# Splitting Wq and normalising the first rows in the context stage, and placing the first unit's maxima among the query projections

## The reference

```python
x = x + attn(layernorm(x), k, v, ...)                  # one head, 2048 keys
x = x + xattn(layernorm(x), ctx, ctx, Wq, bq, Wk, bk, Wv, bv, Wo, bo, mask)
x = x + ffn(layernorm(x), ...)                         # shared expert and top 2 of 8

# xattn: 16 heads of 32; ctx has 4 x 1601 rows
q, k, v = heads(Q @ Wq.T + bq), heads(K @ Wk.T + bk), heads(V @ Wv.T + bv)
scores = where(mask == 0, -1e9, q @ k.T / sqrt(32))
out = (softmax(scores) @ v) @ Wo.T + bo
```

## Time and profile before

| what | us |
|---|---|
| median of 3 runs | 4144.37 |
| lowest, highest | 4143.46, 4153.04 |
| the profiled execution | 4149.81 |
| its span in the trace | 4148.0 |
| TensorE busy | 3834.7 (92%) |
| VectorE busy | 2428.6 (59%) |
| ScalarE busy | 1427.9 (34%) |
| GpSimd busy | 1473.0 (36%) |

### The profile page before, as it was taken

One profiled execution on the slowest core, in us unless ns is written; L12 is line 12 of the kernel. 1 busy time (PEld: TensorE's weight loads), 2 busy tenths in 40 slices (PEclk: granted clock), 3 DMA queues, 4 the chain that ended last, 5 costly groups with the idle time before them and its releaser, 6 DMA issues. The chain is left out here.

```text
span 4148.0 us, 64160 instructions
## 1 busy us (share of the span) xinstructions
PE 3834.7 (92%) x19160; PEld 2567.8 (62%) x19161; DVE 2428.6 (59%) x6243; ACT 1427.9 (34%) x1752; POOL 1473.0 (36%) x806
## 2 busy tenths in 40 slices
PE   4999999979968699999999999999996799997997
PEld 3888888868856344444444444444442677785875
DVE  5444444434437488888878888878883533434235
ACT  2212211222222055455545554545554221212332
POOL 1000000000000177766666666777664212310033
PEclk7999999989988699999999999999998899998999
DMA  3010010045544412222222222222201433228478
GB/s 132 30 38 30 30 38 30 28 136 187 184 146 142 119 37 53 54 53 54 53 54 53 54 53 54 51 53 54 53 6 47 162 102 122 102 71 282 166 278 288
DMA packets 223679, 381.48 MB, mean 92 GB/s; under 512 B 16936, under 2 KB 101448, under 8 KB 223436
## 3 DMA queue, kind: packets, MB, share of 16 engines
q1 hardware_dynamic: 196204, 309.73, 25.6%
q0 software_dynamic: 13120, 43.00, 2.8%
q10 hardware_dynamic: 14112, 25.70, 1.6%
HBM read 229.71 MB, written 148.66 MB: 91 GB/s over the span
## 5 line engine op out<-in xcount | busy, mean ns | idle before, releaser
L1389 DVE CUSTOM_DVE_ANT_0 xa_unread<-xa_mx_ps,mask_q 128x402 bf16<-128x402 f32 x2048 | 1065.7, 573 | 330.2 <-PE xa_mx_ps L1249 192.8
L1356 ACT ACTIVATE xa_prob<-xa_scores 128x1024 f32<-128x1024 f32 (+1 forms) x832 | 834.2, 1023 | 821.6 <-PE xa_scores L1270 808.9
L1229 POOL TENSOR_TENSOR xa_sums<-xa_sums,xa_prob 128x1024 f32<-128x1024 f32 x448 | 1056.8, 2378 | 38.1 <-POOL xa_sums L1229 29.1
L1249 PE MATMUL xa_mx_ps<-xa_kp,xa_qp 96*128 96x402 f32 x2048 | 742.1, 428 | 34.9 <-DMA xa_vg<-values 34.8
L1249 PEld LDWEIGHTS xa_mx_ps<-xa_kp,xa_qp 96*128 96x128 f32 x2048 | 371.2, 192 | 382.7 <-DVE xa_maxima L1389 227.0
L1264 PE MATMUL xa_scores<-xa_qp,xa_kp 97*128 97x512 f32 (+1 forms) x1664 | 568.2, 423 | 14.5 <-issue 6.9
L1270 PE MATMUL xa_scores<-mask_t,ident_b 128*128 128x512 bf16 (+1 forms) x1664 | 549.8, 388 | 0.0
L1278 PE MATMUL xa_o_ps<-xa_prob,xa_vg 128*32 128x512 f32 (+1 forms) x3328 | 449.1, 606 | 3.7 <-issue 3.7
L1264 PEld LDWEIGHTS xa_scores<-xa_qp,xa_kp 97*128 97x128 f32 (+1 forms) x1664 | 296.5, 187 | 156.7 <-ACT xa_prob L1356 90.1
L1229 POOL TENSOR_TENSOR xa_sums<-xa_prob 128x1024 f32<-128x1024 f32 x64 | 151.1, 2380 | 532.3 <-ACT xa_prob L1356 532.3
L1270 PEld LDWEIGHTS xa_scores<-mask_t,ident_b 128*128 128x128 bf16 (+1 forms) x1664 | 122.9, 100 | 242.1 <-issue 207.9
(11 more groups left out here) (276 smaller groups left out, 6105.6 us busy)
## 6 DMA issues: line engine op xcount, KB each, us to landing
xa_kp<-kT_high SPq DMA_DIRECT2D x32, 800.5 KB
ex_src<-sorted_in SPq DMA_DIRECT2D x78, 256.0 KB
sorted_out<-ex_made ACTq DMA_DIRECT2D x78, 256.0 KB
xa_qp<-qT_high SPq DMA_DIRECT2D x32, 512.0 KB
xa_kp<-kT_low SPq DMA_DIRECT2D x16, 800.5 KB
cxl_rows<-in_ctx SPq DMA_DIRECT2D x16, 768.0 KB, 5.2
values<-cxl_v SPq DMA_DIRECT2D x48, 256.0 KB
xa_vg<-values SPq DMA_DIRECT2D x16, 768.0 KB
```

The source lines that it names most:

```text
L1229: pool.tensor_tensor(sums[pr][:, :, :], left[pr][:, :, :], right[pr][:, :, :], ALU.add).then_inc(pool_added, 1)
L1249: pe.matmul(mx_ps[slot % 3][:, 0:MKEYS], qp[par][0:MAXROW, j, first:first + P], kp[par][0:MAXROW, j, MFIRST[kb]:MFIRST[kb] + MKEYS], start ...
L1356: act.activation(prob[ring][pr][0:keys, :, :], scores[pr][0:keys, :, :], ACT.Exp, scale=SCALE).then_inc(exped, 1)
L1389: dve.tensor_tensor_reduce(out=unread[slot % 2][:, :], in0=mx_ps[slot % 3][:, 0:MKEYS], in1=mask_q[:, half * QB + qt, MFIRST[kb]:MFIRST[kb ...
```

## The change

Four things move. Wq is split in the context stage, in the same call as Wk and Wv; that function now waits for each weight by itself and goes around 8 banks. The first two steps' rows of x1 are loaded, and their statistics and normalisation done, in the last batch of the context stage. The query loop is written out instead of looped: it normalises in place in two row buffers, has two PSUM banks for turns instead of four, and gives the low parts of the queries to GpSimd. And the first unit of the cross attention is prepared there: keys and values are loaded at the start, its queries when they are stored, the 64 slots stand three to a chunk from step 2 on, with the reads on VectorE, two banks for them, and the peaks and the row behind. The cross attention then begins with its first score. Memory for the second unit's queries holds the parts of Wq, and two of the four sets of probabilities hold the rows.

```diff
 def split_weights(nc, ident, tag, weights, outs):
+        BANKS = min(len(weights) * DC, 8)
-                pe.wait_ge(loaded, 16 * len(weights))
                 for n, (w, r) in enumerate(cases):
+                    if r == 0:
+                        pe.wait_ge(loaded[w], 16)
+                    if n >= BANKS:
+                        pe.wait_ge(low_done, n - BANKS + 1)
...
 def context_keys_values(...)
-        split_weights(nc, ident, "cxw", [Wk, Wv], [wk, wv])
+        split_weights(nc, ident, "cxw", [Wk, Wv, Wq], [wk, wv, wq])
...
                     load(0, 0)
                     load(0, 1)
+                    for s in range(2):
+                        sp.dma_start(q_rows[s][:, :, :], x_rows[s]).then_inc(q_rows_in[s], 16)
...
                     def body(b, q, following):
                         low_k(b, q, following(1))
                         finish_v(b, q)
                         if q % 2 == 0:
                             preparation.vector(dve, 2 * b + q // 2)
+                        if isinstance(b, int) and q in (1, 2):
+                            normalize_queries(q - 1)
+                        if isinstance(b, int) and q in (0, 1):
+                            query_statistics(q)
```

In `cross_attention` the first loads, the first 64 slots and reads, `peak(0)`, `turn_peaks(0)`, `keep_row(0)` and `set_row(0, 0, 0)` are gone, the semaphores start from the values that they would have left, and GpSimd sets ones in one key buffer there, not two:

```diff
-                load(0, 0)
-                set_row(0, 0, 0)
                 later_loops(sp, unit)
...
-                pe.wait_ge(const, 3)
-                pe.wait_ge(loaded, 16 * LOADS)
-                for slot in range(SLOTS):
-                    mx(0, 0, 0, slot)
-                turn_peaks(0)
...
-                for slot in range(SLOTS):
-                    read(0, 0, slot)
-                peak(0)
```

More of the change, by code:

```diff
@@ L569, in split_weights @@
         rows = sb("rows", [P, len(weights), DC, D])
-        banks = ps("banks", [P, len(weights) * DC, DC, P])
-        loaded, turned, high_done, low_done = sem("loaded"), sem("turned"), sem("high"), sem("low")
+        BANKS = min(len(weights) * DC, 8)
+        banks = ps("banks", [P, BANKS, DC, P])
+        loaded = [sem(f"loaded{w}") for w in range(len(weights))]
+        turned, high_done, low_done = sem("turned"), sem("high"), sem("low")
         cases = [(w, r) for w in range(len(weights)) for r in range(DC)]
@@ L631, in context_keys_values @@
             preparation = MaskPreparation(sb, ps, sem, ident_b, mask, *masks)
+            norm = LayerNorm(sb, sem, BANK // P)
+            q_rows_in, normed = [sem(f"q_rows_in{i}") for i in range(2)], sem("normed")
+            x_rows = x1.rearrange("(s r p) n -> s p r n", p=P, r=BANK // P)
             def even(q):
@@ L720, in _ @@
                         pool.wait_ge(padded, n + 1)
+                    norm.pool_setup(pool)
+                    for s in range(2):
+                        norm.pool_step(pool, s)
                 @block.tensor
@@ L840, in _, with normalize_queries, query_statistics @@
                         low_c(0, 0, r)
+                    def normalize_queries(s):
+                        norm.normalize(dve, q_rows[s], q_rows[s], s).then_inc(normed, 1)
+                    def query_statistics(s):
+                        dve.wait_ge(q_rows_in[s], 16)
+                        norm.statistics(dve, q_rows[s], s)
                     def body(b, q, following):
@@ L1069, with load_keys @@
 PAIRS = GH // 2
-def cross_attention(nc, ident, ident_b, kT, qT, v, mask_q, mask_t, row, oT):
+QB = BANK // P
+MB, MKEYS = 4, 402
+MFIRST = [0, 400, 800, S2 - MKEYS]
+SLOTS = GH * QB * MB
+RING = 4
+MAXROW = 3 * DK
+ROWS97 = MAXROW + 1
+def load_keys(sp, kT, v, i, kp, vg, loaded):
+    for high_or_low, first in ((0, 0), (0, DK), (1, 2 * DK)):
+        sp.dma_start(words(kp[first:first + DK, :, :]),
+                     one(kT[high_or_low], i).rearrange("(j p) n -> p j n", p=DK)).then_inc(loaded, 16)
+    whole = (KT - 1) * P
+    sp.dma_start(vg[:, 0:KT - 1, :], one(v, i)[0:whole, :].rearrange("(t p) n -> p t n", p=P)).then_inc(loaded, 16)
+    sp.dma_start(vg[0:LAST, KT - 1, :], one(v, i)[whole:S2, :]).then_inc(loaded, 16)
@@ new lines, in load_queries, with put_row @@
+def load_queries(sp, qT, i, qp, queries, loaded):
+    for high_or_low, first in ((0, 0), (1, DK), (0, 2 * DK)):
+        sp.dma_start(words(qp[first:first + DK, :, queries]),
+                     one(qT[high_or_low], i).rearrange("(j p) n -> p j n", p=DK)[:, :, queries]).then_inc(loaded, 16)
+def put_row(sp, row, qp, half, row_in):
+    sp.dma_start(words(qp[MAXROW:ROWS97, :, half * BANK:(half + 1) * BANK]),
+                 row.rearrange("(o j t) n -> o j (t n)", o=1, j=GH)).then_inc(row_in, 16)
@@ new lines, in scores_of_slot, with maximum_of_slot @@
+def scores_of_slot(pe, out, qp, kp, half, slot):
+    j, qt, kb = slot // (QB * MB), slot // MB % QB, slot % MB
+    first = half * BANK + qt * P
+    return pe.matmul(out[:, 0:MKEYS], qp[0:MAXROW, j, first:first + P],
+                     kp[0:MAXROW, j, MFIRST[kb]:MFIRST[kb] + MKEYS], start=True, stop=True)
+def maximum_of_slot(dve, scores, mask_q, half, slot, unread, maxima):
+    j_qt, kb, qt = slot // MB, slot % MB, slot // MB % QB
+    return dve.tensor_tensor_reduce(
+        out=unread[slot % 2][:, :], in0=scores[:, 0:MKEYS],
+        in1=mask_q[:, half * QB + qt, MFIRST[kb]:MFIRST[kb] + MKEYS], scale=1.0, scalar=LOWEST,
+        op0=ALU.add, op1=ALU.max, accum_out=maxima[:, j_qt, kb:kb + 1])
@@ L1192, in set_row @@
                     sp.wait_ge(row_out, 16 * (u + 3))
[L1193 to L1194 removed]
+                    put_row(sp, row, qp[par], half, row_in)
                 def store(u, half):
@@ L1221, in _ @@
                 pool.memset(ones[:, :], 1.0).then_inc(const, 1)
-                for i in range(2):
-                    pool.wait_ge(const, i + 1)
-                    pool.memset(words(kp[i][MAXROW:ROWS97, :, :]), 1.0).then_inc(const, 1)
+                pool.wait_ge(const, 1)
+                pool.memset(words(kp[1][MAXROW:ROWS97, :, :]), 1.0).then_inc(const, 1)
+                pool.wait_ge(const, 2)
                 def add(u, kt, left, right):
@@ L1244, in mx @@
                 def mx(u, par, half, slot):
-                    j, qt, kb = slot // (QB * MB), slot // MB % QB, slot % MB
                     m = SLOTS * u + slot
                     pe.wait_ge(mx_read, m + 2)
-                    first = half * BANK + qt * P
-                    pe.matmul(mx_ps[slot % 3][:, 0:MKEYS], qp[par][0:MAXROW, j, first:first + P],
-                              kp[par][0:MAXROW, j, MFIRST[kb]:MFIRST[kb] + MKEYS], start=True, stop=True).then_inc(mx_made, 1)
+                    scores_of_slot(pe, mx_ps[slot % 3], qp[par], kp[par], half, slot).then_inc(mx_made, 1)
                 def turn_peaks(u):
@@ L1388, in read @@
                     dve.sem_inc(carried, 1)
-                    dve.tensor_tensor_reduce(
-           out=unread[slot % 2][:, :], in0=mx_ps[slot % 3][:, 0:MKEYS],
-           in1=mask_q[:, half * QB + qt, MFIRST[kb]:MFIRST[kb] + MKEYS], scale=1.0, scalar=LOWEST,
-           op0=ALU.add, op1=ALU.max, accum_out=maxima[:, j_qt, kb:kb + 1]).then_inc(mx_read, 1)
+                    maximum_of_slot(dve, mx_ps[slot % 3], mask_q, half, slot, unread, maxima).then_inc(mx_read, 1)
                 def peak(u):
```

400 lines of the change are left out of this document (201 added, 199 removed).

## The result

| what | before | changed |
|---|---|---|
| median of the runs | 4144.86 (4) | 4080.7 (4) |
| lowest, highest | 4143.46, 4153.04 | 4075.18, 4084.68 |
| profiled execution, its span | 4149.81, 4148.0 | 4079.72, 4077.9 |
| first score matmul in the trace | 1446.67 | 1383.11 |

The ratio is 0.984, 95% interval 0.9823 to 0.9858: 64.2 us less, against 66 forecast. The first score comes 63.6 us earlier, so the medians leave next to nothing to explain behind it. From the first score to the first hidden-layer product (L44 of `hdl_proj_ps`, at 3216.37 before and 3149.29 after) it is 1769.7 and 1766.2 us, and in two later runs 1768.7 and 1764.9: that much is the difference between executions. The two profiled spans are 70.1 us apart, and 6.5 of that lies behind the first score.

What follows compares the result with a forecast made beforehand. The kernel was taken as a chain of TensorE stages, with idle time from 1203.6 to 1446.67 to gain. Terms put the first score at 1380.1 instead of 1446.7, 66.6 us less: 4078 us, range 4061 to 4095.

Steps and rivals of the forecast that it cites:

- T0 moves: Start of the projection's block comes 6.9 us later, from Wq's split and LayerNorm work in the context stage; bounds 0.4 and 12.
- filling: Start of the projection's block: four turns with their high and low parts before the first products, 6.1 us.
- steps 0 and 1: First two projection steps: 14.4 us with a cold start, then 19.9 with a stall for late rows.
- wait for the queries: TensorE at slot 0 waits 14.2 us for a query load issued behind step 1's stores; bounds 8 and 17.
- steps 2 to 7, with the restart: Later projection steps: 17.6 us each for 2 to 5, bound by VectorE, 1.6 for restart, then 28.5 for the last two.
- tail: From last product to first score: split, stores, row of maxima out and back, and block end, 13.7 us.
- a stall of 5.6 us: In step 1, the fourth turn waits for a low part held on VectorE behind late rows; 1.5 more for the clock.
- rival A: Projection loads land in time: no step 1 stall (7.1 us), query wait only 8; 4065 us, chance 0.17.
- a step costs 12.8 us without a stall: Query projection: four head chunks of 3.2 us each on TensorE, read from the old kernel's timeline.
- Rival C: Projection with slots: TensorE and VectorE take turns instead of overlapping, 121 us more, 4199 us, slower than before; chance 0.02.
- Rival B: Steps 2 to 5: VectorE waits 3.2 us for rows in each, with low-clock restarts in two; 4095 us, chance 0.17.
- Rival D: The projection grows by as much as the start of the cross attention loses; 4144 us, chance 0.02.

Runs made afterwards that it cites:

- four edits: Changed kernel with slot 0's queries loaded earlier, per-step LayerNorm spread and power moved ahead, first LayerNorms one context block later, row of maxima sent before the last stores: 4051.49 us.

## Why the prediction was right, point by point

The likeliest case came, 4078 forecast for 4080.7, and no rival did as a whole. The terms:

| term | forecast | measured |
|---|---|---|
| T0 moves | 6.9 | 5.55 |
| filling | 6.1 | 5.9 (1209.99 to 1215.87) |
| steps 0 and 1 | 34.3 | 34.2 (to 1250.04) |
| wait for the queries | 14.2 | 16.3 |
| steps 2 to 7, with the restart | 100.5 | 103.5 (1266.36 to 1369.8) |
| tail | 13.7 | 13.3 |

The first score comes 3.0 us later than forecast: 1383.1 against 1380.1.

- **Context stage: right mechanism, right size.** TensorE waits for a low part behind the LayerNorm, 3.35 and 0.87 us (forecast 3.2 more than 0.66, and 1.3), and none of it with the work one block later. With the clock behind the first wait that is 5.9 us (330.5 less 324.5, see above), where the sum had 6.5. The weights came out at -0.4 instead of +0.4 (first turn at 873.8, before at 874.2). With 3 us between the profiles of one and the same split, neither sign is shown.
- **Steps 0 and 1: right sum, wrong cause in part.** The step that failed is "a stall of 5.6 us" in step 1 by late rows. The rows were late by 1.32 us on VectorE, and no 5.6 us stall stands in step 1. On this half rival A was right. The 3.57 us at its start come from a chain that I had seen only for later steps: `normalize` waits for GpSimd's power behind the second split, and the step's last low part stands behind both. The steps took 18.4 and 15.8 us where I had 14.4 and 19.9. The two errors cancel in the sum, which is luck. The restart was also undersized: behind the 3.57 us of idle the first chunk of step 1 takes 5.9 us instead of 3.2, so 2.7 and not 1.5.
- **Wait for the queries: right, 2.1 short.** The order of SyncE's program sets it, which early loading proved (14.8 us back). The load did not pass the stores, which rival A needed: it took 8.2 us from issue to landing behind them and 4.2 ahead of them. The split is 1.29 us, not 1.1; the split's end came 4.6 us behind the last product, not 2.9, since VectorE's third and fourth queries stood behind `normalize`; and the three loads took 3.6 us to issue, which I had not counted.
- **Steps 2 to 5: 18.26 against 17.6, and the right engine.** VectorE has 16.5 us of work in 18.2, TensorE 16.0 (forecast 17.0 and 15.4). The rest of VectorE's step is the wait for the power, 0.60 as forecast, and a term that the sum left out: 0.20 before each of the four low parts, for the high part that ScalarE makes. TensorE waits twice in a step for `xf_maxima`, 1.4 and 0.8 us; moving the power made the step 17.56, and spreading the LayerNorm besides 17.05. But "a step costs 12.8 us without a stall" was wrong for this loop: with the slots out it is 17.0, since each first turn waits for a low part at the end of that chain and the clock fell behind every second wait. I had read 12.8 as a sum of TensorE's work, and the 3.4 us wait before the change as the single buffer's. That reading does not hold either. Before the change `normed` was free once the turns that begin at 1250.09 were done, and `normalize` began only at 1254.80, with no idle time before it, behind VectorE's other work. It did no harm to the forecast only because VectorE's own row of work, with its waits, is 18.26 and so longer than the chain. The lines, from the kernel before and then from the change:

```profile
1250.09 0.60 PE L972 MATMUL pql_banks<-ident,pql_normed 128*128 128x128 f32 x4
1254.80 1.90 DVE L883 TENSOR_SCALAR pql_normed<-pql_rows,pql_ln_mean_var,pql_ln_rstd 128x512 f32<-128x512 f32 x4
...
1294.61 0.69 DVE L1149 TENSOR_TENSOR pql_nT_low<-pql_banks,pql_nT_high 128x512 fp32r<-128x512 f32 x1 [0.20 <-ACT pql_nT_high L1122]
1299.65 1.92 DVE L907 TENSOR_SCALAR probs<-probs,pql_ln_mean_var,pql_ln_rstd 128x512 f32<-128x512 f32 x4 [0.60 <-POOL pql_ln_rstd L891]
```

- **Rival C fell for the reason given.** The products cover the reads: twelve slots cost 1.3 us a step among products, and 8.9 by themselves over two banks (12 x 0.74), 6.1 over three (12 x 0.51). Rival B's waits for rows are absent from steps 2 to 5: there `normalize` waits 0.60 us, for the power.
- **Rival D fell.** Nothing came back behind the first score, as the 1765 to 1770 us above show.
- **A split does not hold `normalize`.** The prediction weighed what the Trainium skill, SBUF — State Buffer, Who interferes with whom, says of a VectorE instruction with two SBUF inputs beside a GpSimd one, and priced it at 4.5 us if it should hold for `normalize`. In the change the two never meet. Where GpSimd's power goes ahead of the second split they do, and neither takes longer for it. This pair stands in the kernel of early queries with the power ahead:

```profile
1228.83 1.29 POOL L1053 TENSOR_TENSOR pql_qT_low<-pql_q,pql_qT_high 128x512 fp32r<-128x512 f32 x1 [0.20 <-ACT pql_qT_high L1133]
1229.87 1.90 DVE L907 TENSOR_SCALAR probs<-probs,pql_ln_mean_var,pql_ln_rstd 128x512 f32<-128x512 f32 x4
```

They overlap by 0.25 us (1229.87 to 1230.12), and `normalize` takes 1.90 as elsewhere (1.91, 1.92) and the split 1.29 as elsewhere. That answers it for this instruction over a short overlap. No run here has a VectorE instruction with two tensors from SBUF beside a split.

**Where the 63.6 us come from.** Taken out one at a time, Wq's place is worth 7.4 us and that of the two LayerNorms about 10, each from one profile. That leaves some 46 for the first unit's preparation. This part was not taken out as a whole: the number is a remainder. Some 14 of it come from placing the slots among the products rather than behind them over two banks (26.6 once slot 0 need not wait); the rest is the loads and the waiting that the projection now covers. With the four edits it is 29.8 more (1382.72 to 1352.88).

## What to carry to other kernels

When small dependent work is spread among large products, price its slots by what they add to the step, and find the step's own length from the chain over all engines that ends it, not from the busiest engine's sum. A load that is ready early but stands behind a store in its queue's program waits for that store's producer: move the issue before buying a faster transfer. Put new work on a shared in-order engine behind the instruction that the bound engine waits for, not ahead of it: the same LayerNorm cost 5.9 us in one context block and nothing in the next.

## What the hardware did that I had not expected

- A DMA issue on SyncE takes longer when stores went out just ahead: 1.11 to 1.25 us for a load of queries behind two stores, 0.34 to 0.86 for the same ones issued earlier; and the row's 1.12 us behind stores against 0.34 without. The transfers are the same. Stores are not the whole of it: in the kernel of four edits the low half's load takes 1.23 us with the last store 7 us back. What holds the issue was not tried.
- The row of maxima takes 6.2 us to memory right behind two stores of 1 MB, and 1.8 us when the last ones went out 5 us earlier.
- Slots by themselves over two PSUM banks take 0.74 us each, at a granted clock of 0.55, and over three banks 0.51 at 0.50. Among products over two banks TensorE waits for a read twice a step; three were not tried there.
- The same wait can cost TensorE its clock or not. Behind 1.87 us of idle the first chunk took 3.3 us in the kernel with the slots behind (granted clock 0.97 over that step) and 4.8 in the one with the LayerNorms back (0.65 over that chunk), against 3.2 undisturbed.
